# Score maxima of an attention kernel read from two neighbouring PSUM banks by one VectorE instruction

## What is computed

```python
v = values.reshape(N, Lk, HEADS, HEAD_DIM) @ Wv.T
k = keys.reshape(N, Lk, HEADS, HEAD_DIM) @ Wk.T
q = queries.reshape(N, Lq, HEADS, HEAD_DIM) @ Wq.T
e = jnp.einsum('nqhd,nkhd->nhqk', q, k) / jnp.sqrt(jnp.float32(EMBED))
e = jnp.where(mask == 0, jnp.float32(-1e+20), e)
attn = jax.nn.softmax(e, axis=-1)
out = jnp.einsum('nhqk,nkhd->nqhd', attn, v)
...
x = x + _L1_xattn_ref(ctx_1024, ctx_1024, _layernorm(x, axis=-1), mask_Bx1xSxS2_ik1, ...)
x = x + _L1_ffn_ref(_layernorm(x, axis=-1), ...)
```

## Time and profile before

| | us |
|---|---|
| time, median of 3 runs | 1934.35 (1933.2 to 1935.07) |
| time of the profiled execution | 1934.45 |
| its span, first to last instruction | 1932.7 |
| TensorE busy, matmuls | 1684.9 (87%) |
| TensorE busy, weight loads | 1195.2 (62%) |
| VectorE busy | 1086.5 (56%) |
| ScalarE busy | 754.8 (39%) |
| mean granted clock of TensorE | 0.939 |

### The profile page before, as it was taken

The page is one execution under the profiler, slowest core; times in us unless marked ns, Lnnn a source line. Parts: engine busy times, 40 slices in busy tenths (PEclk is TensorE's granted clock), DMA queues, the critical chain, the costliest instruction groups (busy, mean ns, idle before and its releaser), DMA issues.

```text
span 1932.7 us, 26797 instructions
## 1 busy us (share of the span) xinstructions
PE 1684.9 (87%) x9406; PEld 1195.2 (62%) x9406; DVE 1086.5 (56%) x2262; ACT 754.8 (39%) x1218; POOL 63.5 (3%) x81
## 2 busy tenths in 40 slices
PE   7999998777698777787899999996889889899999
PEld 5666665555444345664677878783748466666666
DVE  4434435788786667778745251616777767432332
ACT  2211212666556544555212222212747566412221
POOL 0000000000000000000000000000000000000000
PEclk9999999888899888899899999998999999899989
DMA  9320003000000000000200000003000000000000
GB/s 307 132 86 0 0 0 129 28 10 10 0 1 1 1 11 11 10 10 0 87 2 2 2 1 2 2 2 120 2 5 5 0 5 0 0 11 0 11 11 11
DMA packets 31785, 49.66 MB, mean 26 GB/s; under 512 B 7998, under 2 KB 27582, under 8 KB 31550
## 3 DMA queue, kind: packets, MB, share of 16 engines
q1 hardware_dynamic: 31198, 37.49, 6.0%
q10 hardware_dynamic: 512, 11.11, 1.7%
HBM read 46.50 MB, written 12.58 MB: 31 GB/s over the span
## 4 chain that ended last, share of the span: by engine, by line
PE 43%; issue 39%; DVE 8%; ACT 4%; DVEq 3%; ACTq 1%; POOL 1%; POOLq 0%; DMA 0%; SPq 0%
PE bank L1648 6%; PE bank L1673 6%; PE bank L1559 6%; PE bank L1560 5%; PE bank L1622 3%; PE bank L1379 3%; DVE plo L718 2%; PE bank L1399 2%; PE bank L1381 2%; PE bank L1333 2%; PE bank L1491 1%; ACT hq L1148 1%; ACTq L1147 1%; ACT phi L1089 1%; PE bank L1516 1%
## 5 line engine op out<-in xcount | busy, mean ns | idle before, releaser
L718 DVE TENSOR_TENSOR plo<-e,phi 120x512 f16<-120x512 f32 x256 | 185.4, 740 | 85.9 <-ACT phi L1089 80.2
L1399 PE MATMUL bank<-Q,Kpad 128*120 128x256 f16 x1024 | 209.2, 287 | 8.6 <-ACT MBT L1081 8.6
L1095 ACT ACTIVATE e<-bank 120x512 f32<-120x512 f32 x256 | 152.7, 597 | 67.7 <-PE bank L1404 37.9
L673 DVE TENSOR_REDUCE MB<-bank 128x4 bf16<-128x480 f32 x256 | 149.9, 648 | 18.4 <-PE bank L1381 12.2
L1089 ACT ACTIVATE phi<-e 120x512 f16<-120x512 f32 x256 | 158.1, 622 | 0.0
L1379 PE MATMUL bank<-Kpad,Q 128*128 128x480 f16 x256 | 108.9, 425 | 55.9 <-issue 32.0
L986 DVE SCALAR_TENSOR_TENSOR x<-bank,gwt,x 128x256 f32 x128 | 56.0, 479 | 158.5 <-PE bank L1673 158.5
L1403 PE MATMUL bank<-MBT,selm 128*120 128x256 bf16 x512 | 143.9, 281 | 0.0
L1404 PE MATMUL bank<-MBT,sels 128*120 128x256 bf16 x512 | 143.6, 280 | 0.0
L1422 PE MATMUL bank<-V,phi 120*128 120x34 f16 (+1 forms) x1024 | 85.4, 176 | 56.2 <-DVE plo L718 54.7
L1648 PE MATMUL bank<-xT,w1e 128*128 128x512 f32 x256 | 124.0, 630 | 3.3 <-DVE gl L956 3.3
(11 more groups left out here) (226 smaller groups left out, 3122.3 us busy)
## 6 DMA issues: line engine op xcount, KB each, us to landing
h1w<-copy_h1T SPq DMA_DIRECT2D x1, 4096.0 KB, 17.8
h2w<-copy_h2T SPq DMA_DIRECT2D x1, 4096.0 KB, 12.9
ctxp<-in_ctxT SPq DMA_DIRECT2D x13, 240.0 KB, 2.7
m<-in_mask SPq DMA_DIRECT2D x9, 240.0 KB, 2.8
w1e<-in_w1e SPq DMA_DIRECT2D x1, 2048.0 KB
w2e<-in_w2e SPq DMA_DIRECT2D x1, 2048.0 KB
out<-x SPq DMA_DIRECT2D x4, 512.0 KB, 2.9
winT<-in_winT SPq DMA_DIRECT2D x1, 2040.0 KB, 14.2
```

The lines of the kernel that those rows point to most:

```text
L673: dve.tensor_reduce(MB[:, t, h0 // 8, SK + h0 % 8:SK + h0 % 8 + 4], bank[2 + n % 4][:, 0:4 * SK].rearrange("p (h k) -> p h k", h=4), AX.X, ...
L718: dve.tensor_tensor(plo[:, u % 3, :], e32[:, u % 3, :], phi[:, u % 3, :], ALU.subtract).then_inc(s.lo, 1)
L1095: act.activation(e32[:, u % 3, :], bank[2 + u % 4][0:SK, :], ACT.Exp).then_inc(s.exp, 1)
L1399: pe.matmul(ps, Kpad[:, v, r, g, b * SK:b * SK + SK], Q2[:, g, qs], start=(v == 0), stop=False)
```

## The change

The eight banks become slices of one PSUM tensor, so that one access pattern can go over two of them. The reduction takes banks 2 and 3, or 4 and 5, at once: 2 x 4 x 120 = 960 columns give eight maxima, and there are half as many. `s.ap` rises once per two banks, after the second; TensorE waits for `s.red` ahead of each second bank's worth of fills, for the reduction that read the same pair of banks. Matmuls, transposes and everything else keep their number and order.

```diff
@@ -42,7 +42,7 @@
         self.sets = heads // 8
         self.pvh = heads // 2
         self.units = heads
-        self.approx = TT * heads // 4
+        self.approx = TT * heads // 8
@@ -252,7 +252,8 @@
-    bank = [es.enter_context(nc.psum_tensor(f"bank{b}", [128, 512], F32)) for b in range(8)]
+    banks = es.enter_context(nc.psum_tensor("banks", [128, 8, 512], F32))
+    bank = [banks[:, b, :] for b in range(8)]
     bankh = [t[:, :].bitcast(BF16) for t in bank]
@@ -664,14 +665,14 @@
                 last.then_inc(s.qlo, 1)
 
-                per = L.heads // 4
+                per = L.heads // 8
                 for t in range(TT):
                     for q in range(per):
                         n = t * per + q
                         dve.wait_ge(s.ap, i * n_ap + (n + 1))
-                        h0 = 4 * q
-                        dve.tensor_reduce(MB[:, t, h0 // 8, SK + h0 % 8:SK + h0 % 8 + 4],
-                                          bank[2 + n % 4][:, 0:4 * SK].rearrange("p (h k) -> p h k", h=4),
+                        b0 = 2 + 2 * (n % 2)
+                        dve.tensor_reduce(MB[:, t, q, SK:SK + 8].rearrange("p (b h) -> p b h", b=2),
+                                          banks[:, b0:b0 + 2, 0:4 * SK].rearrange("p b (h k) -> p b h k", h=4),
                                           AX.X, ALU.max).then_inc(s.red, 1)
@@ -1362,7 +1363,7 @@
                 def transpose_maxima(t):
-                    pe.wait_ge(s.red, i * n_ap + (t + 1) * (L.heads // 4))
+                    pe.wait_ge(s.red, i * n_ap + (t + 1) * (L.heads // 8))
                     if t >= 2:
                         pe.wait_ge(s.mbt, i * TT + (t - 1))
@@ -1372,14 +1373,16 @@
                 for t in range(TT):
                     for q in range(L.heads // 4):
                         n = t * (L.heads // 4) + q
-                        if n >= 4:
-                            pe.wait_ge(s.red, i * n_ap + (n - 3))
+                        if n >= 4 and n % 2 == 0:
+                            pe.wait_ge(s.red, i * n_ap + (n // 2 - 1))
                         g, r0, b = 4 * q // HG, 4 * q % HG, t // 2
                         ps = bank[2 + n % 4][:, 0:4 * SK]
                         pe.matmul(ps, Q2[:, g, tok(t)], Kpad[:, 0, r0:r0 + 4, g, b * SK:b * SK + SK],
                                   start=True, stop=False)
-                        pe.matmul(ps, identb[:], MB[:, t, 0, 0:SK].unsqueeze(1).broadcast_to([128, 4, SK]),
-                                  start=False, stop=True).then_inc(s.ap, 1)
+                        last = pe.matmul(ps, identb[:], MB[:, t, 0, 0:SK].unsqueeze(1).broadcast_to([128, 4, SK]),
+                                         start=False, stop=True)
+                        if n % 2:
+                            last.then_inc(s.ap, 1)
```

## The result

The changed kernel took 1941.41 us, the median of 22 runs (1934.66 to 1947.61), against 1934.24 us for the kernel before (22 runs, 1930.46 to 1936.42): a ratio of 1.0036, 95% interval 1.0025 to 1.0047. It is slower by 7.2 us (4.8 to 9.1). The runs of the changed kernel also scatter over 13 us instead of 6. The profiled execution of the changed kernel was one of the slower ones, 1945.79 us with a span of 1944.0, so it stands 11.3 us above the span of before, and its stages have to be compared one by one, at equal clock.

A forecast was written before the change was run, and what follows sets the result against it. VectorE's reductions were taken to pace the maxima stage, the hand-over after the change. Stage-end losses of 2.2 + 1.0 + 1.2 and 1.7 for L3's last fill, 6.1 us, on 1934.35 gave 1940.5 us; range 1935.0 to 1944.6.

The forecast's parts named there:

- one clock window either way: Spread around the forecast if one half-clock window more or less falls, 1.6 us each: given as 1938.5 to 1942.3 us.
- Part 1: VectorE's maxima reductions: a pair lasts 1.145 us, 1.065 back to back against 1.129; 8.2 us saved if VectorE alone counted.
- Rival (c): Pair reduction costs more than its columns: 1944.3 us as two passes (chance 0.12), 1949 as two full reductions (0.04).
- Part 2: Hand-over between TensorE and VectorE: with two buffers its cycle binds, 2.237 us per four banks against 2.258 before.
- Rival (a): VectorE's floor in the maxima stage is reached after all: 1935.4 us, not slower; chance 0.10.
- Part 3: Two ends of a maxima stage: later pairs lose 2.2, 1.0 and 1.2 us, L3's last fill 1.7 us.
- Part 4: One tensor with slices, changed semaphore rises and waits, queue order: edits that cost nothing.
- Rival (b): Half-clock windows at the start of the scores in L1 and L2 vanish, 4.8 us back: 1935.7 us; chance 0.12.
- the prediction's own last test: Sign that the forecast is wrong: more than two clock windows are redrawn.

The follow-up runs named there:

- e1: Changed kernel, but the approximate scores go round three pairs of banks instead of two: 1940.88 us, ratio 1.0031 to the kernel before.
- e6: Changed kernel with 22 extra matmuls per pass, results unread, to hold TensorE's clock in the stages: 1920.29 us, ratio 0.9914 to the kernel before.
- e3: Changed kernel with single reductions of 480 columns and one tensor per bank again, keeping the change's semaphore hand-over per pair: 1938.30 us, ratio 1.0023 to the kernel before.
- e9: Changed kernel with 22 extra matmuls per pass, both semaphores rising by 2 per pair to count banks: 1921.55 us, ratio 0.9933 to the kernel before.
- e5: Kernel before with 22 extra matmuls per pass, results unread, to hold TensorE's clock in the stages: 1910.40 us, ratio 0.9869 to the kernel before.
- e11: Kernel before with 22 extra matmuls per pass, both semaphores rising by 2 per bank: 1919.53 us, ratio 0.9920 to the kernel before.
- e10: Changed kernel with six banks, singles for each stage's first eight banks, pairs after, 22 extra matmuls per pass, semaphores counting banks: 1903.36 us, ratio 0.9838 to kernel before.
- e4: Kernel before, but VectorE waits until both banks of a pair are filled, each bank still released by itself: 1952.72 us, ratio 1.0088.
- e7: Changed kernel with six banks, single reductions for the first eight banks of a stage, pairs after: 1933.27 us, ratio 0.9983 to the kernel before.

## Why the prediction was right, and where it was not

The forecast was 1940.5 us; 1941.41 came, inside its own range, and slower by an amount whose interval (4.8 to 9.1 us) holds the 6.1. (The bounds 1938.5 and 1942.3 for one clock window either way don't follow from its 1.6 us, which gives 1938.9 and 1942.1; nothing else rests on them.) Point by point:

- **Part 1** held to the nanosecond: 1.145 us, 1.157 after a wait, 1.065 from start to start where nothing else binds (e1). Rival (c) is out. The 125 ns per VectorE instruction on PSUM that the Trainium skill gives, in "Perfetto Trace Analysis", section "Optimizing Scalar/DVE Operations", would have made the floor's gain twice as large. The measurement decides: e1 shows 1.129 - 1.065 = 0.064 us.
- **Part 2** held: 2.237 us for four banks, in the changed kernel and in e6; 2.30 in e3 and 2.305 in e9, each by its own terms. Rival (a) needed the cycle below 2.13; it takes a third pair (e1). The other sentence of the same section of the Trainium skill is that, where VectorE isn't saturated but causes bubbles in other engines, breaking instructions up may finish the work sooner. The ends of a stage agree: with the small reductions the scores of L3X come 1.74 us behind the last one instead of 2.17 (e5 against e6).
- **Part 3** held in the main at equal clock: 0.51, 0.35, 0.40, 0.32 and 0.46 us in the five stages of L1X and L2X whose half-clock time stayed near that of before (0.30 to 0.45 foretold), 0.31, 0.31, 0.17 and 0.14 in L3X (0.38 to 0.21, so the last two fell short), and 0.43 at each end in L3X. In L1X and L2X ScalarE's slice hid the last fill: 0.89 us from last reduction to scores in both.
- **Part 4 failed**: an edit at nothing cost 0.31 us in each of twelve passes, 3.7 us. The prediction weighed where the semaphores rise and where they are waited for, and not the numbers that they are compared with. What the counts multiply decides whether other waits of the program need a register instruction (e11, e9, e10).
- **Rival (b) was sized too small.** It counted windows behind a stage and one window either way. Three stages of L1X and L2X in the profiled run had 5.8 us of half clock at their start instead of 2.7 to 3.1, and grew by 1.15 to 1.31 us; three passes of them began their scores at half clock that had not before, 1.9 us each with the 0.3 in it. In L3X three more stretches from scores to values moved by 1.0 to 1.1 us, one up and two down. By the prediction's own last test, more than two clock windows redrawn, its picture of the clock was wrong. In e4 12 of the 18 us stand outside the stages, with the half-clock time.

So the total was met with one term missing, and that it came within 1 us is partly luck. At equal clock the sum would be 6.1 + 3.7 = 9.8 us, above the measured 7.2 and just above its interval. The 2.6 us between could be windows that fell better on average than in the kernel before; no run shows it. The median of the mean granted clocks of the 22 changed runs is 0.940, the profiled execution of before had 0.939, so the difference would be small. The profiled run of the changed kernel, at 0.935, gives 11.3.

## What to carry to other kernels

One instruction over two buffers halves the number of buffers. Before merging, add up the cycle of one buffer (use, release, fill, start) and compare it with the floor of the engine that is to gain; here 2.24 against 2.13 us took nearly all of the saving, the late start took more than the rest, a third pair brought the pace back (e1), and singles at the start the rest (e7). Here half-clock windows moved times by as much as the edits did, so a comparison of a few us wanted the clock held in both kernels, and even then it was held in the stages alone. And a change of what a semaphore counts needs a look at the register instructions of the waits that share its sums.

## What the runs showed of the hardware

- A reduction over two neighbouring PSUM banks costs its columns alone: 645 to 1145 ns for 480 more columns, 1.04 ns each.
- A register instruction of 40 ns ahead of a wait behind a drain put the next VectorE instruction off by 78 ns (e6 against e5; e11). It stood there only where no reduction waited for the same sum of loop counter and constant: 256 times, 128, 80 or not at all (e6, e9, e10, e5).
- A rise by 2 on the matmul that VectorE waits for and on the reduction itself came with a wait that stands alone, and 0.07 us from landing to start on top of 0.038 (e9, and at the start of the stages of e11).
- 22 matmuls per pass whose results nobody reads made the kernel before faster by 25 us (ratio 0.9869). TensorE ran at 2.4 GHz throughout the stages, of which 46 us had been at 1.2: the mean granted clock of the profiled runs was 0.959 instead of 0.939, which is 158 instead of 239 us at half clock.
